# One-core perceiver block: GpSimd splits the first batch's expert weight tiles 2 and 3, and tile 15 is handled earlier

## What is computed

```python
x = x + cross_attention(layernorm(x), ctx, ctx)     # 16 heads of 32, ctx is 2 x 2048 x 512
x = x + post_norm(self_attention(layernorm(x)) + layernorm(x))
# self attention reshapes [B, S, E] to [B*H, S, D] directly: a "head" is 8 tokens' worth of rows,
# so features must be shuffled between partition groups before and after its softmax
# feed-forward with a router: every token takes the hidden layer of one of 4 experts
expert_idx = argmax(x @ W_router)
h = gelu(einsum('th,ehi->tei', x, W1) + b1)         # W1 is 4 x 512 x 2048
y = layer_norm(onehot-select(h) @ Wo + bo + x)
```

## Time and profile before

| | before |
|---|---|
| median of 3 runs | 515.41 us (515.33 to 515.44) |
| profiled execution: time | 515.1 us |
| profiled execution: span | 513.3 us |
| PE busy | 495.2 us, 96% |
| DVE busy | 307.7 us, 60% |
| ACT busy | 266.2 us, 52% |
| POOL busy | 42.2 us, 8% |

### The profile page before, as it was taken

The page is one execution under the profiler, slowest core; times in us unless marked ns, Lnnn a source line. Parts: engine busy times, 40 slices in busy tenths (PEclk is TensorE's granted clock), DMA queues, the critical chain, the costliest instruction groups (busy, mean ns, idle before and its releaser), DMA issues.

```text
span 513.3 us, 9255 instructions
## 1 busy us (share of the span) xinstructions
PE 495.2 (96%) x3742; PEld 378.2 (74%) x3742; DVE 307.7 (60%) x585; ACT 266.2 (52%) x401; POOL 42.2 (8%) x34
## 2 busy tenths in 40 slices
PE   8999998999999999999999999999899998999995
PEld 6786777777777777897877778757595866877663
DVE  3757532645554553346187384579379978975962
ACT  4230037495857641328357748467345727755730
POOL 0030000000199000000000000000002010000000
PEclk9999999999999999999999999999999999999999
DMA  8900000000341022220310000298387899876001
GB/s 277 357 2 1 1 1 0 2 1 1 108 162 64 1 77 89 82 83 1 106 39 3 0 3 0 68 421 334 109 324 271 316 390 377 298 298 240 1 0 41
DMA packets 11497, 63.52 MB, mean 124 GB/s; under 512 B 1600, under 2 KB 2112, under 8 KB 4544
## 3 DMA queue, kind: packets, MB, share of 16 engines
q1 hardware_dynamic: 11168, 62.67, 32.3%
q10 hardware_dynamic: 288, 0.27, 0.2%
HBM read 62.41 MB, written 0.52 MB: 123 GB/s over the span
## 4 chain that ended last, share of the span: by engine, by line
PE 83%; ACT 7%; DVE 5%; issue 4%; POOL 0%; POOLq 0%; ACTq 0%; DVEq 0%
PE ps L1155 36%; PE ps L1225 11%; PE ps L1239 6%; PE ps L1209 5%; ACT Pm L452 4%; PE ps L1471 3%; PE ps L1473 3%; PE ps L1472 3%; PE ps L1491 3%; PE ps L1430 1%; PE ps L1431 1%; PE ps L1432 1%; PE ps L1149 1%; PE ps L1420 1%; ACT PT L460 1%
## 5 line engine op out<-in xcount | busy, mean ns | idle before, releaser
L753 DVE TENSOR_SCALAR_CACHE_REDUCE Pm<-ps,small 128x512 f32<-128x512 f32 x96 | 66.4, 748 | 30.5 <-PE ps L1209 30.3
L460 ACT COPY PT<-ps 128x512 f32<-128x512 f32 x128 | 68.5, 592 | 28.9 <-PE ps L1225 28.9
L1225 PE MATMUL ps<-ident,Pm 128*128 128x128 f32 x512 | 69.3, 277 | 3.2 <-ACT Pm L452 3.2
L1225 PEld LDWEIGHTS ps<-ident,Pm 128*128 128x128 f32 x512 | 56.5, 141 | 18.0 <-issue 11.0
L452 ACT ACTIVATE Pm<-Pm,small 128x2048 f32<-128x2048 f32 x32 | 64.3, 2011 | 3.5 <-DVE Pm L753 3.5
L733 DVE SCALAR_TENSOR_TENSOR KrL<-ps,small,KrH 128x512 fp32r<-128x512 f32 x32 | 23.9, 747 | 61.2 <-ACT KrH L438 61.2
L1155 PE MATMUL ps<-wvH,ctxH 128*128 128x512 f32 x124 | 50.3, 405 | 1.0 <-DVE V L742 1.0
L1155 PE MATMUL ps<-ctxH,wkH 128*128 128x512 f32 x124 | 51.1, 412 | 0.0
L1155 PE MATMUL ps<-ctxL,wkH 128*128 128x512 f32 x124 | 48.6, 392 | 0.0
L1155 PE MATMUL ps<-ctxH,wkL 128*128 128x512 f32 x124 | 48.5, 391 | 0.0
L1155 PE MATMUL ps<-wvH,ctxL 128*128 128x512 f32 x124 | 48.4, 390 | 0.0
(11 more groups left out here) (229 smaller groups left out, 872.3 us busy)
## 6 DMA issues: line engine op xcount, KB each, us to landing
w1raw<-in_W SPq DMA_DIRECT2D x16, 1024.0 KB, 6.1
w2raw<-in_W SPq DMA_DIRECT2D x16, 1024.0 KB, 7.3
raw<-in_ctxT SPq DMA_DIRECT2D x7, 1024.0 KB, 5.2
woF<-in_ffn_Wo SPq DMA_DIRECT2D x4, 1024.0 KB, 10.0
wo<-in_wo SPq DMA_DIRECT2D x2, 1024.0 KB, 4.9
ctx_first<-in_ctxT SPq DMA_DIRECT2D x4, 256.0 KB, 4.7
wv_raw<-in_xWv SPq DMA_DIRECT2D x2, 512.0 KB, 8.2
wq<-in_xWq SPq DMA_DIRECT2D x1, 1024.0 KB, 13.3
```

Of the source, the lines that this page charges most:

```text
L460: act.copy(PT[:, c % 2, i, :, :].rearrange("p k t -> p (k t)"), ps[:, t_bank(p, c, i), :]).then_inc(pt_done, 1)
L753: dve.tensor_scalar(Pm[:, i, c * CH:(c + 1) * CH], ps[:, i, :], -1.0, mx[:, p % 2, i, c - 1:c] if c else NOT_YET, ALU.mult, ALU.min, accum ...
L1225: last = pe.transpose(ps[:, t_bank(p, c, i), j * P:(j + 1) * P], Pm[:, i, c * CH + j * P:c * CH + (j + 1) * P], ident[:])
```

## The change

Tiles 2 and 3 leave `WHOLE` and are multiplied in three passes. GpSimd makes both their halves, cast and subtraction, and only then casts tiles 8 and 9; the cast of tile 8, which takes over buffer A, now waits for tile 3. VectorE splits the two token tiles first (z23H, z23L). ScalarE's first copy of the second softmax no longer waits for the value shuffles. Tile 15 is loaded before `second_in(1)` and the `rowsF` rows, cast before ScalarE's x2T copies, and subtracted before `logits(1)`.

```diff
-        WHOLE = (0, 1, 2, 3, 14)
+        WHOLE = (0, 1, 14)
+        BY_POOL = (2, 3)
+        z23H = at("z23H", [P, 2, T], F32R, 164)
+        z23L = at("z23L", [P, 2, T], F32R, 25)
...
-        HIGH_OF = {4: "C", 5: "A", 6: "B", 7: "D", 8: "A", 9: "C", 10: "E", 11: "B", 12: "D", 13: "A", 15: "B"}
-        SPLIT = tuple(HIGH_OF)
+        HIGH_OF = {4: "C", 5: "A", 6: "B", 2: "E", 3: "A", 7: "D", 8: "A", 9: "C", 10: "E", 11: "B", 12: "D", 13: "A", 15: "B"}
+        SPLIT = tuple(t for t in HIGH_OF if t not in BY_POOL)
...
+            sp.wait_ge(first_tile, USED[10])
+            first_in_(15)
             second_in(1)
             for n in range(3):
                 sp.dma_start(rowsF[:, n, :], a["rows"][4 + n:5 + n, :].to_broadcast([P, D])).then_inc(rowsF_in, 16)
-            sp.wait_ge(first_tile, USED[10])
-            first_in_(15)
...
-            first_high(8, 5)
+            for n, (t, freed) in enumerate(((2, 4), (3, 5))):
+                if t == 2:
+                    pool.wait_ge(qkv_mm[1], 1)
+                first_high(t, freed)
+                pool.wait_ge(first_hi_pool, n + 1)
+                pool.tensor_tensor(w1L[RAW_OF[t]][:], w1raw[RAW_OF[t]][:], w1H[HIGH_OF[t]][:].bitcast(F32),
+                                   ALU.subtract).then_inc(first_pool, 1)
+            first_high(8, 3)
             first_high(9, 4)
...
                 act.wait_ge(p2T_mm[b], i + 1)
-                if i == 0:
+                if i == 0 and b == 0:
                     act.wait_ge(v2_dve[b], 2 * HPG)
                     act.wait_ge(v2_act[b], 2 * HPG)
...
-            first_high(10, None)
+            first_high(10, 2)
...
             first_high(13, 8)
+            first_high(15, 11)
             transposed(yT[1], x2T_mm, 1, XT_BANKS[1], x2T_done)
             transposed(yTH, x2T_mm, 1, XT_BANKS[1], yT_hi)
-            first_high(15, 11)
...
             dve.tensor_tensor(b1L[:], b1raw[:], b1H[:].bitcast(F32), ALU.subtract).then_inc(b1_lo, 1)
+            step(dve.tensor_copy(z23H[:], z0[:, 2:4, :]))
+            dve.tensor_tensor(z23L[:], z0[:, 2:4, :], z23H[:].bitcast(F32), ALU.subtract).then_inc(z23_split, 1)
             queries2(1)
...
-            dve.wait_ge(first_hi_pool, 1)
+            dve.wait_ge(first_hi_pool, 3)
             first_low(8)
-            dve.wait_ge(first_hi_pool, 2)
+            dve.wait_ge(first_hi_pool, 4)
             first_low(9)
...
+            dve.wait_ge(first_hi_act, 6)
+            first_low(15)
             logits(1)
             router(1)
...
-            dve.wait_ge(first_hi_act, 6)
-            first_low(15)
             onehots_T(1)
...
                 wH, wL = w1H[HIGH_OF[t]], w1L[RAW_OF[t]]
-                zH_, zL_ = z0H[:, SPLIT.index(t), :], z0L[:, t - KT, :]
+                if t in BY_POOL:
+                    pe.wait_ge(z23_split, 1)
+                    pe.wait_ge(first_pool, BY_POOL.index(t) + 1)
+                    zH_, zL_ = z23H[:, t - 2, :], z23L[:, t - 2, :]
+                else:
+                    pe.wait_ge(first_split, 2 + SPLIT.index(t) + 1)
+                    zH_, zL_ = z0H[:, SPLIT.index(t), :], z0L[:, t - KT, :]
```

More of the change, by code:

```diff
@@ L226, in perceiver_block @@
         w1_in = [sem(f"w1_in{i}") for i in range(len(w1_kb))]
-        first_hi_pool, first_hi_act, first_split = (sem(n) for n in ("first_hi_pool", "first_hi_act", "first_split"))
+        first_hi_pool, first_hi_act, first_split, z23_split, first_pool = (
+            sem(n) for n in ("first_hi_pool", "first_hi_act", "first_split", "z23_split", "first_pool"))
         w2_in = [sem(f"w2_in{i}") for i in range(RING2)]
@@ L1423, in first_halves @@
             def first_halves(t):
-                pe.wait_ge(first_split, 2 + SPLIT.index(t) + 1)
                 wH, wL = w1H[HIGH_OF[t]], w1L[RAW_OF[t]]
-                zH_, zL_ = z0H[:, SPLIT.index(t), :], z0L[:, t - KT, :]
+                if t in BY_POOL:
[5 more added lines that the diff above has]
+                    zH_, zL_ = z0H[:, SPLIT.index(t), :], z0L[:, t - KT, :]
                 for c in range(IC):
@@ L1440, in first_experts @@
                 t = FIRST[n]
-                if t < KT:
+                if t < KT and t in WHOLE:
                     pe.wait_ge(z0_done, 1)
```

## The result

The changed kernel takes **531.27 us** (median of 4 runs, 531.05 to 531.79) against 515.42 us: 1.031 times the time before, 95% interval 1.029 to 1.033. It is slower by 15.9 us. I forecast 529.3, range 522 to 532.

A forecast was written before the change was run, and what follows sets the result against it. TensorE, busy 96% of the span, was taken as the bound, so only its work and waits count. 515.1 + 11.3 (held copies) + 1.3 (clock) + 1.9 (tile 8's cast) - 0.3 (end) = 529.3 us, range 522 to 532.

The forecast's parts named there:

- The hold: Before scores2(1): VectorE's QT and KT copies stand still until GpSimd's cast or subtraction ends; scores2(1) +11.3 us.
- One copy per boundary: One held VectorE copy slips in at each GpSimd boundary: 3 done by 389.95, the other 25 to 397.4, scores2(1) at 397.6.
- The z23 rows: Two added VectorE instructions before QT, costed at nothing beside 2.05 us of idle time; about 0.7 us without that gap.
- The clock after the first wait: After the 11 us idle before scores2(1), TensorE runs at half clock through scores2 and part of tile 2: +1.3 us.
- Tile 8's moved cast: GpSimd's cast waits for tile 3, delaying VectorE's subtractions of tiles 8 to 10, its reciprocal and attention2_out: +1.9 us.
- S': Start of scores2(1) in the changed kernel, forecast at 397.6 us.
- S: Start of scores2(1) in the kernel before, 386.24 us.
- The end: TensorE's 0.8 us wait for tile 15 goes, but VectorE's chain is late next: -0.3 us.
- The first: Rival: VectorE wins the turns, copies run back to back, TensorE waits for GpSimd's tiles 2 and 3; 525.5 to 527.5; chance 0.26.
- Side by side: Rival: GpSimd and VectorE run together, copies keep 0.27 us; about 515.0, no change; chance 0.14.
- the partial hold: Rival: GpSimd's casts stop VectorE's copies, its subtractions don't; 517 to 520, up to 524; chance 0.10.

The follow-up runs named there:

- one_subtract: Kernel before plus one extra GpSimd subtraction of 128x2048, result unused, started when batch 1's q is computed; tile 2's product waits for it: 518.12 us, ratio 1.007.
- two_memsets: Kernel before plus two GpSimd memsets of 128x2048, result unused, started when the second batch's q is computed: 518.2 us, a single run.
- split_in_pieces: Changed kernel with each of GpSimd's four instructions for tiles 2 and 3 cut into 8 pieces of 256 columns: 527.77 us, ratio 1.024.
- clock_fillers: Changed kernel with unused identity matmuls in TensorE's two long waits, 46 ahead of scores2(1) and 15 ahead of attention2_out(1): 527.47 us, ratio 1.023.
- late_cast_8: Kernel before with only GpSimd's cast of tile 8 made to wait for tile 3, no GpSimd split: 519.51 to 520.60 us, ratio 1.010.
- pool_after_copies: Changed kernel with GpSimd's four instructions held back until VectorE has made the QT, KT and first VT copies: 528.78 us, ratio 1.027.
- two_memsets_timed: The kernel before with two extra unused GpSimd memsets of 128x2048, run again and timed: 517.86 us, ratio 1.005.

## Why the prediction was right, point by point

- **The hold.** Right, shown by one_subtract (copy against subtraction, which no row of before had), two_memsets and split_in_pieces. The rule of the Trainium skill ("SBUF — State Buffer", section "SBUF: two separate sides"), an exclusive lock on the shared port pair for the whole instruction, agrees with all three.
- **One copy per boundary.** Right, and so is the count: three copies were done when GpSimd's last subtraction ended (390.03), and the fourth, held by it, ended 0.12 us later. scores2(1) came at 397.38 against 397.6. That it is so near is partly luck: 0.5 us of the shift from the earlier trace rows was there before the change's first instruction (GpSimd began at 377.02, not 376.5), and the 0.45 us that I allowed for hand-overs was not needed, since GpSimd's four instructions took 13.0 us with their gaps. Without that earlier 0.5 us the term measured 10.6 and not 11.3 us.
- **The z23 rows.** Costed at nothing, and right: VectorE still idled 1.38 us before QT.
- **The clock after the first wait.** +1.3 forecast. Tile 3 ended 9.54 us after scores2(1)'s start, 8.0 without the loss by the forecast and 7.96 in clock_fillers: +1.5.
- **Tile 8's moved cast.** +1.9 forecast. attention2_out(1) started at S' + 27.6, of which 1.5 is the clock: 1.7 measured, and clock_fillers, at S' + 26.06 against S + 24.4, gives the same 1.7. The run late_cast_8 shows that this edit alone is a loss.
- **The end.** -0.3 forecast. The tile behind attention2_out(1) began 16.14 us later than before (429.81 against 413.67), batch 1's first product 15.84 later (449.11 against 433.27): -0.3.
- **What the sum lacked**: a second clock loss. I forecast a wait of some 3.5 us before attention2_out(1), and it is 3.4, but I priced the clock only after the long wait. attention2_out(1) took 4.80 us in place of 3.03: +1.8. With it the terms are 0.5 + 10.6 + 1.5 + 1.7 + 1.8 - 0.3 = 15.8, the difference of the spans. This is nearly all of the 2 us by which 531.27 lies above 529.3. In the trace of the kernel before TensorE idles from 507.1 and the clock is still 1.00 at 509 to 511 (the stretch between the two of the earlier trace rows), and I read from it that waits under 4 us are free. A wait of this length may cost clock or not: the profiled execution of pool_after_copies had the same wait and no loss, so a forecast without this term could have been met as well.
- **The rivals.** The first has its mechanism wrong: VectorE never won two turns. Where its schedule was forced (pool_after_copies), attention2_out(1) came at 421.14 (forecast 421.3) and that execution took 525.60 us, but the median of 528.78 lies 1.3 above its range of 525.5 to 527.5, which allowed 2 us for the clock. Side by side and the partial hold are ruled out.

## What to carry to other kernels

Before giving GpSimd a part of VectorE's work, list what VectorE does in that stretch. In these traces SBUF copies and subtractions of two SBUF tiles stand still for the length of each GpSimd instruction, while operations that read PSUM go on at 0.69 us. One 1644 ns maximum in a group with a median of 266 was the whole warning. Small edits that shorten waits may gain while the large edit beside them loses (514.1 against 531.1 us), so time them apart.

## What I had not expected of the hardware

Short waits can cost clock. In two_memsets TensorE waited 1.9 us, at full granted clock, and the clock fell after work had resumed:

```profile
384.00:388.00 4.00, 2.45 (x11) 1.00 0.88 320
390.00:392.00 2.00, 2.00 (x3) 0.50 0.28 111
394.00:396.00 2.00, 2.00 (x12) 1.00 0.11 16
```

In the profiled execution of one_subtract it waited 2.1 us and the clock stayed at 1.00, and waits of 3.44 and 3.45 us before the same product lost it in the change and kept it in pool_after_copies. So the length of the wait alone does not decide it. In two_memsets_timed three of four runs of one kernel seem to have lost it where one did not. That is read from the mean clock of each run, a rough sign: one_subtract took 518.04 us at 0.993 and 518.12 at 0.998. What does decide it these runs leave open. Each loss that a trace shows cost 1.5 to 1.8 us. Also new to me: a memset, which reads nothing, holds VectorE's copies (1.84 us in place of 0.27), and turns between the two engines alternate, one instruction each, down to pieces of 0.4 us.
